# The maximum of a slot: turned by VectorE in 32 by 32 blocks instead of by TensorE

## The reference, cut to what matters

```
q = (layernorm(x) @ wq.T + bq)            # per head: 128 queries x 32
k = (ctx @ wk.T + bk);  v = (ctx @ wv.T + bv)   # per head: 2048 keys x 32
scores = q @ k.T / sqrt(32)
attn = softmax(scores)                    # exp(scores - m) / sum, over 2048 keys
x = x + (attn @ v) @ wo.T + bo
```

## Time and profile before

| | |
|---|---|
| median of 3 executions | 1685.7 us |
| the profiled execution | 1685.17 us, span 1683.3 us |
| TensorE matmuls busy | 1612.5 us, 96% of the span |
| VectorE busy | 1165.5 us, 69% |
| ScalarE busy | 953.6 us, 57% |
| GpSimd busy | 922.0 us, 55% |
| mean granted TensorE clock | 0.98 |

### The profile page before, as it was taken

One profiled execution on the slowest core, in us unless ns is written; L12 is line 12 of the kernel. 1 busy time (PEld: TensorE's weight loads), 2 busy tenths in 40 slices (PEclk: granted clock), 3 DMA queues, 4 the chain that ended last, 5 costly groups with the idle time before them and its releaser, 6 DMA issues. The chain is left out here.

```text
span 1683.3 us, 37014 instructions
## 1 busy us (share of the span) xinstructions
PE 1612.5 (96%) x15589; PEld 1307.8 (78%) x15604; DVE 1165.5 (69%) x1502; ACT 953.6 (57%) x1445; POOL 922.0 (55%) x490
## 2 busy tenths in 40 slices
PE   7999999999999999999999999677998899999999
PEld 6788888888888888888888888566886677777787
DVE  5137888888888888888888887756433677653322
ACT  4347777777777777776777776753202777630000
POOL 0026788878878888887887886322000344522220
PEclk9999999999999999999999999888999999899999
DMA  5232222222222222222222211203423111211001
GB/s 187 68 54 38 36 38 37 38 39 41 36 36 41 39 37 37 38 39 37 42 36 36 39 29 61 74 3 108 158 87 94 52 51 52 66 51 51 26 25 51
DMA packets 310132, 88.62 MB, mean 53 GB/s; under 512 B 259376, under 2 KB 291888, under 8 KB 309968
## 3 DMA queue, kind: packets, MB, share of 16 engines
q1 hardware_dynamic: 309968, 86.26, 22.3%
HBM read 71.60 MB, written 14.61 MB: 51 GB/s over the span
## 5 line engine op out<-in xcount | busy, mean ns | idle before, releaser
L712 POOL TENSOR_TENSOR b_acc<-b_acc,b_s 128x1024 f32<-128x1024 f32 x168 | 562.7, 3349 | 12.4 <-ACT b_s L958 5.5
L996 DVE TENSOR_TENSOR b_s<-b_s,b_mb 128x2048 f32<-128x2048 f32 x128 | 397.3, 3105 | 31.8 <-ACT b_mb L926 31.8
L1032 DVE TENSOR_TENSOR b_mx<-b_psS,b_mx 128x512 f32<-128x512 f32 x480 | 330.7, 689 | 101.5 <-PE b_psS L798 88.4
L958 ACT ACTIVATE b_s<-b_s 128x2048 f32<-128x2048 f32 x128 | 244.3, 1909 | 14.4 <-DVE b_s L996 11.4
L975 ACT ACTIVATE b_s<-b_psS 128x2048 f32<-128x2048 f32 x128 | 241.2, 1884 | 15.3 <-DVE b_mx L1032 15.3
L43 PE MATMUL b_work<-wvT,cT 128*128 128x512 f32 x496 | 203.3, 410 | 0.0
L43 PE MATMUL b_work<-cT,wkT 128*128 128x512 f32 x496 | 200.3, 404 | 1.7 <-POOL b_ones L678 1.7
L44 PE MATMUL b_work<-cT,wkT 128*128 128x512 f32 x496 | 194.3, 392 | 0.0
L44 PE MATMUL b_work<-wvT,cT 128*128 128x512 f32 x496 | 194.3, 392 | 0.0
L45 PE MATMUL b_work<-wvT,cT 128*128 128x512 f32 x496 | 193.5, 390 | 0.0
L45 PE MATMUL b_work<-cT,wkT 128*128 128x512 f32 x496 | 193.2, 390 | 0.0
(11 more groups left out here) (311 smaller groups left out, 2812.2 us busy)
## 6 DMA issues: line engine op xcount, KB each, us to landing
cin<-in_ctx SPq DMA_DIRECT2D x480, 64.0 KB, 2.4
experts_sb<-in_L_ffn_expert_w SPq DMA_DIRECT2D x8, 1024.0 KB, 5.3
q_scratch<-d_st SPq DMA_DIRECT2D x16, 256.0 KB, 2.3
k_scratch<-d_st SPq DMA_DIRECT2D x16, 256.0 KB, 2.3
e_q<-q_scratch SPq DMA_DIRECT2D x16, 256.0 KB, 2.7
k_sb<-k_scratch SPq DMA_DIRECT2D x16, 256.0 KB, 3.0
cin<-in_ctx SPq DMA_DIRECT2D x4, 512.0 KB, 8.3
b_kT<-in_x SPq DMA_DIRECT2D x4, 512.0 KB, 7.7
```

The source lines that it names most:

```text
L712: nc.gpsimd.tensor_tensor(acc[:, :, :], acc[:, :, :], s[:, buf, 2 * i:2 * i + 2, :], ALU.add).then_inc(sum_done, 1)
L958: nc.scalar.activation(part, part, ACT.Exp, scale=SCALE).then_inc(exp_done, 1)
L996: nc.vector.tensor_tensor(s[:, n % BUFS, :, :], s[:, n % BUFS, :, :], mb[:, :].rearrange("p (o n) -> p o n", o=1).broadcast_to([P, CHUNK, ...
L1032: nc.vector.tensor_tensor(mx[:, :, :], part, mx[:, :, :], ALU.max).then_inc(mx_done, 1)
```

## The change

For the first 28 slots (m < TAIL), TensorE no longer turns mx and VectorE no longer reduces from PSUM. Instead, directly after the last maximum of chunk 3, VectorE does the whole of it, by `slot_maximum`:

1. it transposes mx within 32 by 32 blocks, 128x512, into `spread` (used as scratch before it is filled as before);
2. it reduces each block of 32 columns to one, 128x512 to 128x16, into `part_top[:, 0]`: queries now lie on the partitions, 32 at a time, and each group of 32 partitions holds the part of the maximum from its own 32 key positions;
3. three copies bring the parts of partitions 32 to 63, 64 to 95 and 96 to 127 to partitions 0 to 31, 32x16 each;
4. a second reduction, 32x64 to 32x16, joins the four parts into `row_top`;
5. four copies of 32x4 spread it over the four groups of partitions of `top`.

That is ten instructions: one transpose, two reductions and seven copies, with a wait between one step and the next and one for the last maximum ahead of them. The last four slots do as before. top_done now counts 4 for each of the first 28 slots (function `tops`). The units "M" of these slots leave the ring of banks.

```
@@ -556,7 +560,7 @@
-            if (s0 := turned_slot(beat)) is not None:
+            if (s0 := turned_slot(beat)) is not None and s0 >= TAIL:
                 enter(("M", s0, 0), beat)
@@ -872,7 +883,7 @@
-                if (m := turned_slot(beat)) is not None:
+                if (m := turned_slot(beat)) is not None and m >= TAIL:
                     turn("M", m, mx, mx_done, (m + 1) * MAXIMA)
@@ -949,7 +960,7 @@
-                    act.wait_ge(top_done, m + 1)
+                    act.wait_ge(top_done, tops(m + 1))
@@ -984,6 +995,28 @@
+            def slot_maximum(m):
+                dve.wait_ge(mx_done, (m + 1) * MAXIMA)
+                reached(dve, mb_done, m)
+                nc.vector.transpose(spread[:, :, :], mx[:, :, :]).then_inc(blocks_turned, 1)
+                dve.wait_ge(blocks_turned, m + 1)
+                reached(dve, row_done, m)
+                nc.vector.tensor_reduce(part_top[:, 0, :], spread[:, :, :].rearrange("p j (o c) -> p (j o) c", c=32),
+                                        AX.X, ALU.max).then_inc(part_done, 1)
+                dve.wait_ge(part_done, m + 1)
+                for a in range(1, 4):
+                    nc.vector.tensor_copy(part_top[0:32, a, :], part_top[32 * a:32 * (a + 1), 0, :]).then_inc(gathered, 1)
+                dve.wait_ge(gathered, 3 * (m + 1))
+                reached(dve, top_done, 4 * m)
+                nc.vector.tensor_reduce(row_top.rearrange("p j o -> p (j o)"),
+                                        part_top[0:32, :, :].rearrange("p a n -> p n a"), AX.X, ALU.max).then_inc(row_done, 1)
+                dve.wait_ge(row_done, m + 1)
+                reached(dve, spread_done, m - 1)
+                for o in range(4):
+                    nc.vector.tensor_copy(top[32 * o:32 * (o + 1), m % 2, :], row_top[:, :, o]).then_inc(top_done, 1)
@@ -997,7 +1030,7 @@
-                if (m := spread_slot(beat)) is not None:
+                if (m := spread_slot(beat)) is not None and m >= TAIL:
@@ -1026,10 +1059,14 @@
                         if n % CHUNK == 0 and t == 0:
+                            reached(dve, blocks_turned, min(n // CHUNK, TAIL))
                             nc.vector.tensor_copy(mx[:, :, :], part).then_inc(mx_done, 1)
+                    if n % CHUNK == CHUNK - 1 and n // CHUNK < TAIL:
+                        slot_maximum(n // CHUNK)
```

More of the change, by code:

```diff
@@ L537, in cross_attention, with tops @@
         TILES = B - 1
+        def tops(slots):
+            return 4 * slots if slots <= TAIL else 3 * TAIL + slots
         def late_units(table, beat):
@@ L582, in cross_attention @@
         top = sb("b_top", [P, 2, HG])
+        part_top = sb("b_part_top", [P, 4, HG * 4])
+        row_top = sb("b_row_top", [32, HG, 4])
         spread = sb("b_spread", [P, HG, P])
@@ L605, in cross_attention @@
         top_done = sem("b_top_done")
+        blocks_turned = sem("b_blocks_turned")
+        part_done = sem("b_part_done")
+        gathered = sem("b_gathered")
+        row_done = sem("b_row_done")
         spread_done = sem("b_spread_done")
@@ L754, in wait_evicted @@
                     elif kind == "M":
-                        pe.wait_ge(top_done, m + 1)
+                        pe.wait_ge(top_done, tops(m + 1))
                     elif kind == "W":
```

## The result

The changed kernel takes 1730.4 us in the median of four executions (1730.0 to 1735.9) against 1685.9 (1685.7 to 1686.3): a ratio of 1.0276, 95% interval 1.0263 to 1.0289, 44.5 us slower. The forecast was 1722.8, slower, by copies that take turns with GpSimd. The sign and the mechanism held; 37.1 us were forecast for 44.5. In the profiled executions the last score group of cross attention starts 44.9 us later than before (1167.2 against 1122.3), and what follows it takes as long as before (561.2 against 561.0), so the whole loss lies in cross attention.

What follows compares the result with a forecast made beforehand. TensorE, fully busy in cross attention, was taken as the bound. Copies queueing behind GpSimd delay it 1.41 us in 27 slots, and the first slot gains 0.43: 1685.2 + 27 x 1.41 - 0.43 = 1722.8 us, range 1681 to 1748.

Steps and rivals of the forecast that it cites:

- The gain: TensorE, cross attention: dropping its transposes of mx in 28 of 32 slots saves 0.43 us a slot, 12.0 us.
- Copies queue like L212: VectorE's small SBUF copies wait for GpSimd's instructions at a shared port; slower, 1690 to 1750 us, chance 0.79.
- rival (a): VectorE's copies don't use the port shared with GpSimd; no stall, the 0.43 us is kept, 1673 us; chance 0.16.
- The walk: VectorE's queue after chunk 3's last maximum, followed to TensorE: copies wait for GpSimd, +1.41 us a slot in 27 slots.
- S1: TensorE's second score group of the next slot, at 560.98 us before; forecast at 562.39, +1.41 us a slot.
- What was to be seen: Changed profile: copies of 1 to 2.3 us beside GpSimd, subtraction alone at 2.28, TensorE waiting some 50 us in all.
- Rival (c): VectorE becomes the bound by sheer load; a 6 us block costs 1.1 us a slot, 1715 us; chance within 0.79.

Runs made afterwards that it cites:

- e1: Changed kernel with all seven small copies done as reductions over an axis of length one: 1677.8 us, ratio 0.9935 to the kernel before.
- e4: Changed kernel with GpSimd leaving out six of its seven additions a slot: 1678.4 us, ratio 0.9961 to the kernel before.
- e9: Kernel before with one stray 32x16 reduction and one stray copy added on VectorE in the first 28 slots: 1685.1 us, ratio 0.9998.
- e6: Changed kernel, copies kept, with the block placed behind the subtraction of chunk 3 instead of ahead of it: 1754.4 us, ratio 1.0401 to the kernel before.
- e3: Changed kernel with only the last four copies done as reductions: 1704.2 us, ratio 1.0103 to the kernel before.
- e7: Changed kernel with all seven copies as reductions and the block behind the subtraction of chunk 3: 1699.3 us, ratio 1.0090 to the kernel before.
- e2: Changed kernel with only the first three copies done as reductions: 1718.2 us, ratio 1.0186 to the kernel before.
- e5: Kernel before with GpSimd leaving out six of its seven additions a slot: 1685.1 us, ratio 1.0002 to the kernel before.
- e8: Changed kernel with all seven copies as reductions and the block used in all 32 slots: 1677.3 us, ratio 0.9942 to the kernel before.

## Why the prediction was right, and where it was short

- *The gain*, 0.43 us a slot, was right: e1 and e4 have a period of 31.96 us against 32.40, and TensorE at 800 of 800 us.
- *Copies queue like L212.* This was the choice on which the sign hung, held at 0.79 against 0.16 for rival (a): open beforehand, as no row had such a copy. e9 settles it for 32x16 with a single copy, and e1 and e4 show that the whole loss hangs on it. Rival (a)'s own time, 1673, came out as 1678 in the runs where either the copies (e1) or the additions beside them (e4) are taken away.
- *The walk.* Block from the last maximum to the subtraction 6.02 us forecast, 5.99 measured; subtraction alone, 2.28 against 2.29; 1.41 us a slot in all, 1.43 measured by the period. Single steps were off by hundredths: the small operations take 0.16 as assumed, but follow each other after 0.19; only the second copy waits, and the third follows it at once; of the last four the first begins to wait at 571.26 and the others follow. These errors cancel.
- *Total short by 7.4 us*, the difference between 44.5 and 37.1. The sum had no term for TensorE's clock. The changed kernel in four slots, and one of them on TensorE:

```profile
445.10:448.30 3.20, 3.20 (x10) 2.48 (x9) 3.10 (x6) 1.37 (x1) 2.93 (x2) 0.52 0.49 78
649.90:653.10 3.20, 3.20 (x9) 2.44 (x9) 3.10 (x5) 1.30 (x1) 2.85 (x2) 0.52 0.52 81
820.60:823.80 3.20, 3.20 (x10) 2.49 (x9) 3.10 (x6) 1.37 (x1) 2.92 (x2) 0.53 0.50 78
1025.40:1028.60 3.20, 3.20 (x9) 2.50 (x8) 3.10 (x5) 1.20 (x1) 2.76 (x2) 0.53 0.52 84
...
443.40 1.17 PE L809 MATMUL b_psS<-b_q,b_kT 32*128 32x128 f32 x32 [1.68 <-ACT b_s L986]
444.51 0.62 PE L43 MATMUL b_work<-wvT,cT 128*128 128x512 f32 x1
...
452.35 1.17 PE L809 MATMUL b_psS<-b_q,b_kT 32*128 32x128 f32 x32
```

  In each of these stretches the granted clock is about half, the lower of its two levels (1.2 instead of 2.4 GHz), right behind a stall of S1. The projection matmul that took 0.50 at 581.57 in another slot takes 0.62 here, the next ones 0.63 instead of 0.39, and the following score group comes 8.95 us after S1 (443.40 to 452.35) instead of 7.34 (580.47 to 587.81): 1.6 us, four times, 6.4 us. With the 0.02 us a slot (0.5 us) that is 6.9 of the 7.4. By the last score group the account closes better: 27 x 1.43 - 0.43 + 6.4 = 44.6, and 44.9 were measured. e6 bears it out: the clock falls to 0.50 in seven of its slots, each 1.6 us longer (in the slot shown above it is the stretch from 554.70 to 557.90, where the projection matmuls take 0.63 again), and 27 x 2.16 - 0.43 + 7 x 1.6 = 69.1, where its last score group starts 69.3 us later than before. I had written that TensorE waits and had priced the wait alone.

```profile
554.70:557.90 3.20, 3.20 (x9) 2.37 (x8) 3.12 (x3) 3.10 (x4) 2.79 (x2) 0.50 0.42 65
```

- *What was to be seen.* It all came, some of it smaller: a copy of 2.30 us beside L723 and one of 0.87 beside L692 (1 to 2.3 was forecast), the subtraction alone, the waits at S1 (57.1 - 12.4 = 44.7 us, "some 50" was forecast, and 1.69 in a slot for "about 1.8"), GpSimd's second addition at 2.38 instead of 4.34.
- *Rival (c)*, VectorE at its load limit, is excluded by e1: VectorE is busy 734.95 of 800 us there, about as much as in the changed kernel (740.48), and TensorE doesn't wait. Its sum was off as well: 6 us of work, less 0.6 taken away and 4.5 idle, leave 0.9 us a slot and some 1709 us, not 1.1 and 1715.

What stays open: e1 and e4 ended 3 and 2 us above their forecasts although their slots run as forecast. The last score group of e1 starts 12 us earlier than before (1110.2 against 1122.3), and what follows it takes 5 us longer (566.0 against 561.0). So it is in the profiles of e3, e4 and e7 (565.9 to 566.0) and e2 (567.7), while e5, e6, e9 and the changed kernel have 561.1 to 561.2, as before; e8 has 564.4. There the granted clock differs, in the stretch with the self attention, in the kernel before and in e1:

```profile
1320.00:1420.00 100.00, 96.08 (x775) 76.53 (x783) 75.40 (x197) 76.78 (x350) 44.34 (x75) 0.98 0.16 49
```

```profile
1308.00:1408.00 100.00, 96.17 (x738) 76.58 (x747) 70.63 (x187) 71.35 (x327) 40.84 (x71) 0.92 0.15 49
```

Executions of e1 with a mean clock of 0.98 took 1669.9 to 1672.0 us, those with 0.973 or 0.974 took 1677.7 to 1678.5; beside them the kernel before took 1683.1 to 1685.8 at 0.98 and 1687.6 to 1690.9 at 0.975. Between the medians at about equal clock e1 is 13.7 and 12.5 us faster, near the 28 x 0.43 of the transposes. Why the code behind the changed stage gets the lower clock in five of eight executions of e1, and in three of eleven of the kernel before, wasn't tried.

## What to carry to other kernels

A copy from SBUF to SBUF on VectorE, even one of 32x16 or 32x4, is to be priced with the GpSimd instruction that may run beside it, and a chain of such copies with several of them. Reductions (0.145 to 0.161 us in e1), block transposes (0.694 to 0.702) and the copy out of PSUM (L1029, 0.645 to 0.647 in 24 slots of the kernel before, beside GpSimd's L712 in the earlier trace rows) didn't wait. An idle share of 14% said little about a block placed in front of others in a queue: walk the one chain that leads from it to the engine that bounds, and compare its length with the room there. And where a change makes the full TensorE stall, count the clock besides the stall.

## What the runs showed that I had not expected

- A move of 32x16 or 32x4 by a reduction over an axis of length one takes 0.145 to 0.161 us, no more than the copy (0.157 to 0.167 undisturbed), and the block made of such reductions beats both kernels: 1677.8 us, ratio 0.9935.
- Two small operations within the same partitions overlap (129.84 and 129.92 in e9, also 548.69 and 548.77, the first 0.16 long), while those that change the group of 32 partitions start 0.03 us after the end of the one before (three in 0.54, four in 0.69 in e1). The rule of the Trainium skill named in the prediction (VectorE: DVE Perf Modes, two Vector instructions with no wait between them) agrees with this.
- The clock fell in four slots of the changed kernel, with stalls of 1.7 us in each slot, and in seven slots of e6, with stalls of up to 2.7 us, but in none of the first 28 slots of e2 and e3, where TensorE waited 35.4 us in 24 slots and 27.1 in 25, 1.5 and 1.1 us each. What decides in which slots it falls is open.
